# Side work in other places of the order, small steps and element-wise passes on GpSimd, q kept once

## The chip, the cores and the metric

The kernel runs on one core of a Trainium2 chip. The metric is the time on the device of one execution, in microseconds (us). It was measured three times: 1782.32, 1785.84 and 1788.01 us. The engines are TensorE (PE in the profile; PEld is its weight load), VectorE (DVE), ScalarE (ACT), GpSimd (POOL) and SyncE (SP), which here only issues DMAs.

## The reference

Two attention layers follow each other on x of shape (8, 256, 32, 32). N is 1024 positions, C is 256 channels.

```python
# layer 0: 8 heads of 32 channels, one bias matrix per head, residual
xn = (x - mean) / sqrt(var + eps) * gamma            # over the channels
q, k, v = split(w_qkv @ xn)
sim  = einsum('bhdi,bhdj->bhij', q, k) * scale + bias   # bias: a small MLP on relative positions
attn = softmax(sim, axis=-1)
x = w_out @ einsum('bhij,bhdj->bhdi', attn, v) + x
# layer 1: one head, f and g of 32 channels, h of 256
f, g, hh = Wf @ x + bf, Wg @ x + bg, Wh @ x + bh
attn = softmax(f.T @ g, axis=rows)
x = gamma * (hh @ attn) + x
```

## The kernel before, in words

All eight batches are done one after the other, and each in two groups g of four heads. A group has two phases of 32 steps. In its **rows** phase, step m takes one head's tile of 128 queries by 1024 keys. PE computes the tile (lines 581 and 582), DVE adds the bias and takes the minimum of the negated sum (line 1005, the custom instruction with its accumulator read), and ACT exponentiates it for the row sum (line 819). This phase only gives each row's shift: the row's maximum plus the logarithm of its sum. In the **columns** phase, step n computes the scores again, transposed (line 602: 128 keys by 512 queries of two heads), with the shift in two extra rows of `q_stack`. DVE adds the bias (1019), ACT exponentiates (836), and after every two steps PE multiplies with v (629) for the two steps that lie two pairs back.

The four phases of a batch are called g0 rows, g0 columns, g1 rows and g1 columns here. Everything else is **side work**. The tables `side_0`, `column_0`, `side_1` and `column_1` say at which step of which phase each piece is issued, and every engine walks through the same tables (`side_work`), so the order on each engine is fixed by hand. Layer 1 of batch b-1 runs beside batch b, and the normalisation, q and k of batch b+1 too:

- normalisation of the next x: `mean` and `var` on PE (407), `centre` on DVE (863), `square` on ACT (701), `rstd` on ACT (710 the logarithm, 706 the exponential), `norm` on DVE (869);
- q and k: a product on PE (407, 450), a high part rounded by ACT (714, 718, 722, 726) and a low part by DVE (872, 876, 880, 886). The two parts lie in the buffer `st`, go to DRAM (`q_out`, `k_out`) and come back in another layout (`q_in`, `k_in`);
- v: PE (460), copied by ACT (732); output projection `proj`: PE (472), `add_x` on DVE (894);
- layer 1: f and g on PE (407, 484), high on ACT (736, 740), low on DVE (903); h on PE (496), `keep_h` on DVE (931); then per tile `s1` PE (511), `max1` DVE (943), `exp1` ACT (761), `invert` DVE (947), `scale_h` ACT (770) and four `sa` products on PE (527); `add_y` on DVE (954);
- the shift: logarithm and its inverse's exponential on ACT (748, 750), six small instructions of 128x16 on DVE (913 to 925), a transposition on PE (`turn`, 566), a copy on ACT (`keep_rows`, 756) and two small DMAs (341).

PSUM has eight banks. Score tiles take pairs of them in turn: banks 0 and 2 in rows phases, 0, 2 and 6 in columns phases. Bank 4 and 5 hold side work and the sums with v. Before the first step lies a setup (bias MLP, the bias lines through DRAM, q and k of batch 0), and behind the last a tail: layer 1 of batch 7 alone.

## Time and profile before

| what | value |
|---|---|
| median of three executions | 1785.84 us |
| the profiled execution | 1790.26 us |
| its span, first to last instruction | 1788.5 us |
| setup, up to the first DVE step | 98.5 us |
| batch 0; batches 1 to 6 together; batch 7 | 187.7; 1236.8; 194.8 us |
| tail | 70.7 us |
| mean granted TensorE clock | 0.934 |

The profiled execution took 1.8 us more than its span. It lies 4.4 us above the median. Boundaries of phases are the starts of the DVE's first step in each.

### The profile page before, as it was taken

How to read it: one execution, taken by the hardware profiler on the slowest of the kernel's cores; microseconds unless marked ns; L12 is line 12 of the kernel's file. 1: busy time of each engine (PE TensorE's matmuls, PEld its weight loads, DVE VectorE, ACT ScalarE, POOL GpSimd, SP SyncE). 2: the span in 40 equal slices, each digit the busy share in tenths (PEclk: the TensorE clock that was granted, in tenths of full speed). 3: DMA queues.
4: the chain of work that ended last, by engine and by line, in shares of the span. 5: the costliest groups of instructions: out<-in, count | busy, mean ns of one | idle time of the engine just before them, and what ended most of it. 6: DMA issues, size and time to landing. Idle time of an engine off the chain costs nothing.

```text
span 1788.5 us, 18614 instructions
## 1 busy us (share of the span) xinstructions
PE 1589.6 (89%) x5976; PEld 753.9 (42%) x5976; DVE 1477.8 (83%) x2168; ACT 1382.2 (77%) x2033; POOL 7.1 (0%) x5
## 2 busy tenths in 40 slices
PE   6078899899998999889998999989998999999988
PEld 2043335345353544435453443535444453535424
DVE  3067988898988989898888989899889989899853
ACT  2067889788888878878787888878798887889743
POOL 1000000000000000000000000000000000000000
PEclk9577869999999999999999999999999999999999
DMA  5941204320350203501151203502043203400100
GB/s 129 248 138 36 59 1 132 93 59 1 100 148 1 60 1 107 142 25 35 48 165 37 59 1 107 142 1 60 25 124 101 60 1 90 136 1 0 39 10 23
DMA packets 57257, 122.71 MB, mean 69 GB/s; under 512 B 21428, under 2 KB 22964, under 8 KB 57160
## 3 DMA queue, kind: packets, MB, share of 16 engines
q1 hardware_dynamic: 54344, 115.37, 23.5%
q10 hardware_dynamic: 2816, 6.16, 1.3%
q8 instruction: 47, 0.77, 0.2%
q14 instruction: 50, 0.41, 0.1%
HBM read 78.92 MB, written 44.13 MB: 69 GB/s over the span
## 4 chain that ended last, share of the span: by engine, by line
PE 51%; DVE 24%; issue 18%; DMA 3%; ACT 3%; DVEq 0%; ACTq 0%; SPq 0%
DVE biased L1005 13%; PE psum L527 9%; PE psum L602 9%; PE psum L629 8%; PE psum L581 6%; PE psum L407 6%; DVE biased L1019 5%; PE psum L582 4%; PE psum L450 4%; DMA q_stack<-q_parts 2%; PE psum L460 2%; PE psum L484 1%; ACT probs L836 1%; DVE probs L931 1%; DVE x L954 1%
## 5 line engine op out<-in xcount | busy, mean ns | idle before, releaser
L1005 DVE CUSTOM_DVE_ANT_0 biased<-psum,bias_lines_sb 128x1024 f32<-128x1024 f32 x512 | 617.1, 1222 | 174.1 <-PE psum L582 163.0
L819 ACT ACTIVATE biased<-biased,nmax 128x1024 f32<-128x1024 f32 x512 | 587.4, 1148 | 162.5 <-DVE nmax L1005 157.9
L836 ACT ACTIVATE probs<-biased 128x1024 f32<-128x1024 f32 x512 | 536.8, 1057 | 128.6 <-DVE biased L1019 107.5
L1019 DVE TENSOR_TENSOR biased<-psum,bias_lines_sb 128x1024 f32<-128x1024 f32 x512 | 597.8, 1216 | 45.7 <-PE psum L602 33.4
L602 PE MATMUL psum<-q_stack,k_stack 98*128 98x512 f32 x1024 | 392.8, 490 | 38.5 <-DVE nmax L1005 15.9
L581 PE MATMUL psum<-k_stack,q_stack 96*128 96x512 f32 x512 | 331.1, 647 | 102.5 <-DMA q_stack<-q_parts 46.8
L602 PEld LDWEIGHTS psum<-q_stack,k_stack 98*128 98x128 f32 x1024 | 178.9, 200 | 328.8 <-issue 150.8
L629 PE MATMUL psum<-probs,vT 128*32 128x512 f32 x2048 | 285.1, 627 | 6.2 <-DVE st L886 3.9
L581 PEld LDWEIGHTS psum<-k_stack,q_stack 96*128 96x128 f32 x512 | 100.0, 195 | 287.1 <-DVE nmax L1005 165.8
L582 PE MATMUL psum<-k_stack,q_stack 96*128 96x512 f32 x512 | 210.8, 412 | 0.0
L527 PE MATMUL psum<-probs 128*128 128x512 f32 x384 | 186.6, 592 | 0.0
L582 PEld LDWEIGHTS psum<-k_stack,q_stack 96*128 96x128 f32 x512 | 102.7, 201 | 50.7 <-issue 47.4
L819 ACT ACTIVATION_READ_ACCUMULATOR biased<-biased,nmax 128x1 f32 x512 | 96.0, 188 | 0.0
L450 PE MATMUL psum<-xn,wqkvT 128*128 128x512 f32 x128 | 76.9, 694 | 21.4 <-DVE st L880 7.8
L527 PEld LDWEIGHTS psum<-probs 128*128 128x128 f32 x384 | 72.5, 189 | 46.0 <-issue 36.1
L629 PEld LDWEIGHTS psum<-probs,vT 128*32 128x32 f32 x2048 | 42.6, 109 | 101.3 <-issue 73.5
L761 ACT ACTIVATE probs<-probs,nmax 128x1024 f32<-128x1024 f32 x48 | 54.9, 1144 | 16.4 <-DVE probs L943 15.6
L407 PE MATMUL psum<-xn,wqkvT 128*128 128x512 f32 x128 | 66.3, 599 | 0.0
L460 PE MATMUL psum<-wqkvT,xn 128*128 128x256 f32 x256 | 65.7, 378 | 0.0
L496 PE MATMUL psum<-whT,x 128*128 128x256 f32 x256 | 65.4, 380 | 0.1
L472 PE MATMUL psum<-o,woutT 128*128 128x512 f32 x128 | 64.4, 592 | 0.8 <-ACT o L782 0.8
L527 PE MATMUL psum<-o,probs 128*128 128x512 f32 x128 | 64.8, 592 | 0.0
(78 smaller groups left out, 1090.9 us busy)
## 6 DMA issues: line engine op xcount, KB each, us to landing
q_stack<-q_parts SPq DMA_DIRECT2D x90, 256.0 KB, 5.3
k_stack<-k_parts SPq DMA_DIRECT2D x45, 512.0 KB, 7.3
q_parts<-st SPq DMA_DIRECT2D x15, 1024.0 KB, 3.9
k_parts<-st SPq DMA_DIRECT2D x15, 1024.0 KB, 4.3
xn<-in_x_dram SPq DMA_DIRECT2D x8, 1024.0 KB, 8.9
x<-in_x_dram SPq DMA_DIRECT2D x8, 1024.0 KB, 9.6
out_dram<-x SPq DMA_DIRECT2D x8, 1024.0 KB, 4.1
bias_lines_sb<-bias_lines SPq DMA_DIRECT2D x32, 240.0 KB, 15.1
```

The lines of the kernel that those rows point to most:

```text
L407: mm = pe.matmul(psum[0:rows, bank + half, :], lhsT(k), src[:, k, half * HALF:(half + 1) * HALF], start=(k == 0), stop=(k == KC - 1))
L450: mm = pe.matmul(psum[:, bank, :], wqkvT[:, k, t * C:t * C + P], xn[:, k, half * HALF:(half + 1) * HALF], start=(k == 0), stop=(k == KC - 1))
L460: mm = pe.matmul(psum[:, 4 + arg % 2, 0:C], xn[:, k, arg * P:(arg + 1) * P], wqkvT[:, k, 2 * C:3 * C], start=(k == 0), stop=(k == KC - 1))
L527: mm = pe.matmul(psum[:, 4 + 2 * c + half, :], hs[:, t % HS, c * P:(c + 1) * P], attn1[t % 3][:, half * HALF:(half + 1) * HALF], start=(t ...
L581: pe.matmul(psum[:, bank, :], lhsT, keys[:, 0:HALF], start=True, stop=True)
L582: pe.matmul(psum[:, bank + 1, :], lhsT, keys[:, HALF:N], start=True, stop=True).then_inc(SEMS["a_mm"], 1)
L602: mm = pe.matmul(psum[:, bank + i, :], k_stack[:, g, 2 * j + i, t * P:(t + 1) * P], q_stack[:, g, half, 2 * j + i, :], start=True, stop=True)
L629: mm = pe.matmul(psum[h * HD:(h + 1) * HD, 4 + half, :], vT[:, t, (g * HG + h) * HD:(g * HG + h + 1) * HD], probs[:, ((q - PV_LAG) * HP + ...
L819: nc.scalar.activation(biased[:, m % BIASED, :], biased[:, m % BIASED, :], ACT.Exp, scale=-1.0, bias=nmax[:, m:m + 1], accum_out=rowsum[:, ...
L836: nc.scalar.activation(probs[:, n % P_SLOTS], biased[:, n % BIASED, :] .rearrange("p (i n) -> p i n", i=2), ACT.Exp).then_inc(SEMS["probs_ ...
L1005: nc.vector.tensor_tensor_reduce(biased[:, m % BIASED, :], pair(bank_of(g, first, ("rows", m))), bias_lines[:, g * HG + h, a0:a0 + N], -1. ...
L1019: nc.vector.tensor_tensor(biased[:, n % BIASED, :].rearrange("p (i n) -> p i n", i=2), psum[:, bank:bank + 2, :], bias_lines[:, g * HG + 2 ...
```

## The change

- **GpSimd takes over** the six small shift instructions but the rounding, which DVE keeps: four GpSimd instructions stand before it (a fused one is split in two) and two behind it. It also takes `norm`, and the bias of h (`keep_h`), which ACT now copies out of PSUM first.
- **Two new GpSimd steps** add the two halves of x's channels and of the squares, so that `mean` and `var` each need 2 products of 512 columns and not 4.
- **q of group 1, k of group 1, f, `centre` and the logarithm of the variance** are done in halves of 512. k of group 1 is computed one batch ahead. `st` is now `st_q` and `st_k`. `q_stack` is held once and not once per group; its halves are loaded apart, each as soon as the scores before it have been read.
- **High and low parts** stand one step apart; before, it was two (three for `low_g`).
- **The rows phase of g0** has three pairs of banks for its scores (0, 2, 6). A table `SIDE_BANK` gives every piece of side work its bank, and it waits for the piece that had the bank before.
- **h** is in the last steps of g0 rows, in g0 columns and at the start of g1 rows. Its products fill a bank in pairs, its copy takes 512 columns, and `scale_h` writes in place. `s1` comes every 3 steps from step 3, before it was every 8/3 steps from step 6.
- **In g0 columns** the squares are at steps 0 and 1, `var` at 7 and 10, the norm at 12, the first copy of h at 0 and g at 2, 3, 13 and 14. In g1 columns stand the second half of k of group 0 and all of q of group 0 and k of group 1: five products of two steps each, where there were two. The rounding of the shift is at step 4 and its transposition at step 8 (before 6 or 7).
- **In the setup** the bias lines of heads 2 to 7 are no longer loaded ahead of q and k of batch 0, but behind them.

```diff
+        side_0 += [(11 + a, "q1", a) for a in range(QUANTA)]
+        side_0 += [(12 + 2 * half, "high_q1", half) for half in range(NHALF)]
+        side_0 += [(13 + 2 * half, "low_q1", half) for half in range(NHALF)]
-            at = 6 + 8 * t // 3
+            at = 3 + 3 * t
...
+            slots = S_SLOTS if g == 0 else 2
-            banks = [(0, 2)[(n - columns) % 2] for n in range(columns)]
+            banks = [(0, 2, 6)[(n - columns) % slots] for n in range(columns)]
...
+        def q_in(eng, b, g, half):
             need(eng, "q_stored", b, 16 * (g + 1))
-            need(eng, *done)
+            need(eng, "s_mm", b - 1 + g, (SN if g == 0 else 0) + (half + 1) * (SN // NHALF))
...
+            lines_out(0)
+            bias_in(0)
+            bias_in(1)
+            lines_out(1)
+            for half in range(NHALF):
+                need(sp, f"q_loaded_{half}", 0, Q_DMAS)
+            need(sp, "k_loaded", 0, K_DMAS)
+            bias_in(2)
+            bias_in(3)
+            k_out(sp, 0, 1)
+            k_in(sp, 0, 1)
+            for h in range(HG, G * HG):
+                bias_in(h)
...
+                    nc.scalar.copy(hT[:, 2 * arg:2 * arg + 2, :],
+                                   psum[:, SIDE_BANK["h", arg, b], :]
+                                   .rearrange("p (t c) -> p t c", c=C)).then_inc(SEMS["h_kept"], 1)
...
+            def do(kind, arg, b, g):
+                if kind == "sum_x":
+                    nc.gpsimd.tensor_tensor(x_sum, xn[:, 0, :], xn[:, 1, :], ALU.add).then_inc(SEMS["x_summed"], 1)
+                elif kind == "sum_squares":
+                    nc.gpsimd.tensor_tensor(square_sum, squares[:, 0, :], squares[:, 1, :],
+                                            ALU.add).then_inc(SEMS["squares_summed"], 1)
+                elif kind == "norm":
+                    nc.gpsimd.tensor_tensor(xn[:, arg, :], xn[:, arg, :], rstd, ALU.mult).then_inc(SEMS["normed"], 1)
+                elif kind == "shift":
+                    u = g * NHALF + arg
+                    cols = slice(arg * HM, (arg + 1) * HM)
+                    need(pool, "ln_ready", b, 2 * u + 2)
+                    nc.gpsimd.tensor_tensor(invsum[:, cols], rowsum[:, cols], invsum[:, cols],
+                                            ALU.mult).then_inc(SEMS["scaled"], 1)
+                    need(pool, "scaled", b, 3 * u + 1)
+                    nc.gpsimd.tensor_tensor(lnsum[:, cols], lnsum[:, cols], invsum[:, cols],
+                                            ALU.add).then_inc(SEMS["scaled"], 1)
+                    need(pool, "scaled", b, 3 * u + 2)
+                    nc.gpsimd.tensor_scalar(lnsum[:, cols], lnsum[:, cols], -1.0, None,
+                                            ALU.add).then_inc(SEMS["scaled"], 1)
+                    need(pool, "scaled", b, 3 * u + 3)
+                    need(pool, "a_max", b, g * A_TILES + (arg + 1) * HM)
+                    nc.gpsimd.tensor_tensor(shift[:, cols], nmax[:, cols], lnsum[:, cols],
+                                            ALU.subtract).then_inc(SEMS["shifted"], 1)
+                elif kind == "split_shift":
+                    u = g * NHALF + arg
+                    cols = slice(arg * HM, (arg + 1) * HM)
+                    need(pool, "split_hi", b, u + 1)
+                    need(pool, "shift_mm", b, u - 1)
+                    nc.gpsimd.tensor_copy(shift_parts[:, arg, 0], shift_hi[:, cols].bitcast(F32))
+                    nc.gpsimd.tensor_tensor(shift_parts[:, arg, 1], shift[:, cols], shift_hi[:, cols].bitcast(F32),
+                                            ALU.subtract).then_inc(SEMS["parts_ready"], 1)
+                elif kind == "keep_h":
+                    need(pool, "h_kept", b, arg + 1)
+                    nc.gpsimd.tensor_tensor(hT[:, 2 * arg:2 * arg + 2, :], hT[:, 2 * arg:2 * arg + 2, :], bh_all[:],
+                                            ALU.add).then_inc(SEMS["h_ready"], 1)
...
+                elif kind == "round_shift":
+                    need(dve, "shifted", b, u + 1)
                     nc.vector.tensor_copy(shift_hi[:, cols], shift[:, cols]).then_inc(SEMS["split_hi"], 1)
```

DVE at the start of the g0 columns of a middle batch, before:

```order
L1019 TENSOR_TENSOR biased<-psum,bias_lines_sb 128x1024 x4
L869 TENSOR_TENSOR xn<-xn,o 128x1024
L1019 TENSOR_TENSOR biased<-psum,bias_lines_sb 128x1024
L913 TENSOR_TENSOR invsum<-rowsum,invsum 128x16
L916 SCALAR_TENSOR_TENSOR lnsum<-invsum,lnsum 128x16
L919 TENSOR_TENSOR shift<-nmax,lnsum 128x16
L922 CAST shift_hi<-shift 128x16
L924 COPY shift_parts<-shift_hi 128x16
L925 TENSOR_TENSOR shift_parts<-shift,shift_hi 128x16
L1019 TENSOR_TENSOR biased<-psum,bias_lines_sb 128x1024 x3
L903 SCALAR_TENSOR_TENSOR fg_stack<-psum,bfg,fg_stack 32x512
```

And now, up to the end of that phase (L1137 is the old L1019, L1040 the old L903, L1048 the rounding):

```order
L1137 TENSOR_TENSOR biased<-psum,bias_lines_sb 128x1024 x5
L1048 CAST shift_hi<-shift 128x16
L1137 TENSOR_TENSOR biased<-psum,bias_lines_sb 128x1024
L1040 SCALAR_TENSOR_TENSOR fg_stack<-psum,bfg,fg_stack 32x512
L1137 TENSOR_TENSOR biased<-psum,bias_lines_sb 128x1024 x11
L1040 SCALAR_TENSOR_TENSOR fg_stack<-psum,bfg,fg_stack 32x512
L1137 TENSOR_TENSOR biased<-psum,bias_lines_sb 128x1024 x15
```

The norm and five of the small instructions are gone from DVE, and so are the two low parts of k that followed in this phase; the first low part of g comes after 6 steps instead of 8.

PE at the last steps of the g0 rows of a middle batch, before (L581 and L582 are the scores, L407 the mean of squares, which is `var`):

```order
L581 MATMUL psum<-k_stack,q_stack 128x512
L582 MATMUL psum<-k_stack,q_stack 128x512
L407 MATMUL psum<-x,wfgT 96x512
L407 MATMUL psum<-st,mean_w 128x512
L581 MATMUL psum<-k_stack,q_stack 128x512
L582 MATMUL psum<-k_stack,q_stack 128x512
L407 MATMUL psum<-st,mean_w 128x512
L581 MATMUL psum<-k_stack,q_stack 128x512
L582 MATMUL psum<-k_stack,q_stack 128x512
L407 MATMUL psum<-st,mean_w 128x512
```

And now (L665 and L666 are the scores, L573 f, L520 the mean of x, L586 h):

```order
L573 MATMUL psum<-x,wfgT 96x512
L665 MATMUL psum<-k_stack,q_stack 128x512
L666 MATMUL psum<-k_stack,q_stack 128x512
L520 MATMUL psum<-st_k,mean_w 128x512
L665 MATMUL psum<-k_stack,q_stack 128x512
L666 MATMUL psum<-k_stack,q_stack 128x512
L520 MATMUL psum<-st_k,mean_w 128x512
L665 MATMUL psum<-k_stack,q_stack 128x512
L666 MATMUL psum<-k_stack,q_stack 128x512
L586 MATMUL psum<-whT,x 128x256 x2
```

`var` has left this phase for the g0 columns, the mean stands in its place with half the products, and the first products of h are here.

SP from the storing of the bias table on, before:

```order
L369 DMA bias_lines<-bias_table 8064x1x32 x2
L357 DMA bias_lines_sb<-bias_lines 32x1920 x32
L297 DMA q_parts<-st 128x2x1024
L310 DMA q_stack<-q_parts 32x4x512 x6
L381 DMA xn<-in_x_dram 128x2x1024
```

And now:

```order
L436 DMA bias_lines<-bias_table 8064x1x32
L429 DMA bias_lines_sb<-bias_lines 32x1920 x8
L436 DMA bias_lines<-bias_table 8064x1x32
L429 DMA bias_lines_sb<-bias_lines 32x1920 x8
L388 DMA k_parts<-st_k 128x2x1024
L395 DMA k_stack<-k_parts 32x4x1024 x3
L429 DMA bias_lines_sb<-bias_lines 32x1920 x16
L374 DMA q_parts<-st_q 128x2x1024
L463 DMA xn<-in_x_dram 128x2x1024
```

Twenty-four of the 32 loads of bias lines moved behind the loads of q and k, which ACT issues, and so they now stand in front of the store of q for group 1 and the load of the next x.

## Rows read from the trace of the kernel before

**Rows 1.** The page: each engine's busy time, share of the span and instructions.
```profile
PE 1589.6 (89%) x5976; PEld 753.9 (42%) x5976; DVE 1477.8 (83%) x2168; ACT 1382.2 (77%) x2033; POOL 7.1 (0%) x5
```
**Rows 2.** Windows: the four phases of batch 3 in order (clock and DMA last).
```profile
699.90:754.80 54.90, 50.05 (x169) 27.71 (x165) 47.13 (x79) 45.79 (x81) 0.00 (x0) 1.00 0.43 116
754.80:802.10 47.30, 42.22 (x196) 16.76 (x196) 43.27 (x45) 37.89 (x44) 0.00 (x0) 0.96 0.04 14
802.10:862.30 60.20, 58.26 (x193) 32.20 (x192) 51.62 (x103) 52.04 (x92) 0.00 (x0) 1.00 0.15 35
862.30:905.30 43.00, 40.23 (x188) 15.32 (x188) 41.37 (x45) 35.65 (x39) 0.00 (x0) 0.92 0.37 111
```
**Rows 3.** Groups of instructions in g0 rows of batch 3 (busy, mean ns | idle).
```profile
L1005 DVE CUSTOM_DVE_ANT_0 biased<-psum,bias_lines_sb 128x1024 f32<-128x1024 f32 x32 | 38.5, 1221 | 7.6 <-PE psum L582 7.0
```
**Rows 4.** Timeline, g1 rows of batch 3: step 10, and steps where PE is late.
```profile
818.56 1.22 DVE L1005 CUSTOM_DVE_ANT_0 biased<-psum,bias_lines_sb 128x1024 f32<-128x1024 f32 x1
...
824.13 0.39 PE L582 MATMUL psum<-k_stack,q_stack 96*128 96x512 f32 x1
824.36 1.88 PE L527 MATMUL psum<-probs 128*128 128x512 f32 x4
824.67 1.22 DVE L1005 CUSTOM_DVE_ANT_0 biased<-psum,bias_lines_sb 128x1024 f32<-128x1024 f32 x1 [0.68 <-PE psum L582]
...
825.93 1.15 ACT L819 ACTIVATE biased<-biased,nmax 128x1024 f32<-128x1024 f32 x1 [0.67 <-DVE nmax L1005]
826.31 0.39 PE L582 MATMUL psum<-k_stack,q_stack 96*128 96x512 f32 x1
```
**Rows 5.** Timeline: start of g0 columns of batch 3.
```profile
757.27 2.02 ACT L836 ACTIVATE probs<-biased 128x1024 f32<-128x1024 f32 x2
760.37 1.21 DVE L869 TENSOR_TENSOR xn<-xn,o 128x1024 f32<-128x1024 f32 x1
761.50 1.22 DVE L1019 TENSOR_TENSOR biased<-psum,bias_lines_sb 128x1024 f32<-128x1024 f32 x1
762.64 0.16 DVE L913 TENSOR_TENSOR invsum<-rowsum,invsum 128x16 f32<-128x16 f32 x1
763.63 3.48 DVE L1019 TENSOR_TENSOR biased<-psum,bias_lines_sb 128x1024 f32<-128x1024 f32 x3
```
**Rows 6.** Timeline: ACT's high, DVE's low, in g1 columns of batch 3.
```profile
887.05 0.58 ACT L722 ACTIVATE st<-psum 128x512 fp32r<-128x512 f32 x1
888.77 0.68 DVE L880 SCALAR_TENSOR_TENSOR st<-psum,st 128x512 fp32r<-128x512 f32 x1
889.36 15.92 DVE L1019 TENSOR_TENSOR biased<-psum,bias_lines_sb 128x1024 f32<-128x1024 f32 x14
```
**Rows 7.** GpSimd's longest and a short instruction (timeline).
```profile
0.34 0.11 POOL L1099 MEMSET const-uint8-127<- 128x1 uint8 x1
0.74 6.92 POOL L852 MEMSET k_stack<- 2x8192 f32 x1 [0.29 <-POOLq L1099]
```
**Rows 8.** The chain that ended last, setup.
```profile
51.69 14.38 DMA q_parts<-st
68.36 28.51 DMA q_stack<-q_parts
```
**Rows 9.** DMA between 38 and 97 us.
```profile
DMA packets 11740, 14.18 MB, mean 240 GB/s; under 512 B 9052, under 2 KB 9052, under 8 KB 11740
bias_lines_sb<-bias_lines SPq DMA_DIRECT2D x32, 240.0 KB, 15.1
```
**Rows 10.** Timeline: the tail's f and g.
```profile
1728.67 3.67 PE L407 MATMUL psum<-x,wfgT 128*96 128x512 f32 x8 [0.78 <-DVE x L894]
1738.99 3.73 PE L484 MATMUL psum<-x,wfgT 128*96 128x512 f32 x4 [1.55 <-DVE fg_stack L903]
```
**Rows 11.** Windows: batches 1 to 6; g1 rows of batch 0.
```profile
286.20:1523.00 1236.80, 1149.63 (x4465) 554.45 (x4464) 1100.28 (x1614) 1029.93 (x1518) 0.00 (x0) 0.97 0.24 67
202.40:246.70 44.30, 36.46 (x82) 15.11 (x81) 38.79 (x71) 38.83 (x68) 0.00 (x0) 0.59 0.20 46
```

606 lines of the change are left out of this document (330 added, 276 removed).

## The prediction

> **What bounds the kernel now.** I read the page first. PE is busy for 89% of the span, DVE for 83%, ACT for 77% and GpSimd for 7 us in all [rows 1]. No engine is full, so shares alone decide nothing. Next the windows of one steady batch [rows 2]. The reader is to see that its four phases differ. g0 rows take 54.9 us with DVE busy for 47.1. g0 columns take 47.3 with DVE busy for 43.3. g1 rows take 60.2 with PE busy for 58.3, and g1 columns 43.0 with DVE busy for 41.4. In g0 rows DVE's row tiles stood idle for 7.6 us, 7.0 of them behind PE's score tile [rows 3]. The timeline of g1 rows shows the same in detail: from one score tile to the next PE needs 2.18 us (824.13 to 826.31), because two `sa` products lie between, and DVE waits 0.68 us for a tile that costs it 1.22 [rows 4]. So the rows phases are held by PE's side work and by a ring of only two bank pairs, the columns phases by DVE.
>
> Prices come from distances between starts. A score tile in the columns costs DVE (15.92-0.09)/14 = 1.13 us, a low part of 512 columns 0.59 (888.77 to 889.36) [rows 6]. ACT takes 0.96 for a column step (two in 2.02, one of which ends 1.06 after its start) [rows 5]. A norm, like any pass of DVE over 1024 columns, takes 1.13 (760.37 to the next step at 761.50), the six shift instructions 0.99 (762.64 to 763.63) [rows 5]. A row step takes about 1.15 on DVE and on ACT when nothing is late [rows 4]. On PE, eight passes of 512 columns in float32 take 3.67 us with the last one's end, 0.44 each; a product of 512 columns is two passes, 0.88 [rows 10]. A pass of the scores takes half of that, 0.23 (824.13 to 824.36, the next product being on the spot), a tile of two 0.46 [rows 4].
>
> **The change, phase by phase, for a batch in the middle.**
>
> *g0 rows, 54.9 us.* PE loses 10 products of 512 columns (q and k had 8 and q now has 4; mean and var had 8 and the mean now has 2) and gains two tiles of h, 0.88 each: 8.8 - 1.8 = 7.0 us less, 43.1 of busy time instead of 50.1 [rows 2, 10]. Three bank pairs let it run one tile further ahead. DVE loses a low part (two of 1024 columns become two of 512, -1.1 us) and the shift but the rounding (-0.8), and pays 0.3 for f and `centre` in halves: 47.1 - 1.6 = 45.5. The work of PE no longer outlasts it, so I let the 7 us behind PE go. What is late next is ACT: a low part now stands one step behind its high part, not two. DVE's next row tile ends 1.15 us after the last, but ACT needs the 1.15 of its own exponential and then about 0.6 for the high part [rows 6], which leaves DVE some 0.7 us of idle time. There are four such places here (two of q, two of f), 2.8 us. 45.5 + 2.8 + 0.4 = 48.7.
>
> *g0 columns, 47.3 us.* DVE loses two norms (2.3), 0.8 of the shift and two halves of k (1.2): 43.3 - 4.3 = 39.0. ACT gains two squares (1.9 at 0.95 each by the distance of rows 5), three copies of h (1.4 at the 0.5 of a 512-wide instruction) and loses two high parts (1.1): 37.9 + 2.2 = 40.1. PE's passes sum to 38: scores 14.3, v 14 x 0.88, and 10.5 for g, `var`, half of k and four tiles of h, 0.9 for the next row tiles. So all three come close together. The first steps decide. ACT does two exponentials, a copy and two squares before its third exponential, GpSimd then adds the squares, and PE waits at step 7 for the low part of g before it may write `var` into the same bank. I count 5 us of stops over the phase (before: 47.3 - 43.3 = 4): 39.0 + 5 = 44.
>
> *g1 rows, 60.2 us.* Six of the eight tiles of h (5.3 us) have left PE here, and DVE loses `keep_h` (8 of some 0.3, by the 0.59 of twice the width) and 0.8, and gains half a low part of k. The `sa` products stay: 32 x 0.88 = 28.2 us, now over 25 steps instead of 22. PE's work from the first `sa` on is 25 x 0.46 + 28.2 + six `s1` at 0.46 = 42.4, and the old stretch (41.0 by the same sum, 22 steps) took 43.7, from 818.6 to 862.3 [rows 2, 4]. With the same 2.7 on top, 45.1. The seven steps ahead of it, with two `max1` and one low part, are nine DVE instructions of 1.15, 0.6 and one wait: 11.7. Sum 56.8; the end of one and the start of the other overlap, so I take 56.
>
> *g1 columns, 43.0 us.* DVE gains three halves (1.8) and loses 0.8; five low parts now come one step after the high part, up to 0.5 us each, and PE has 3 more products in pairs of neighbouring steps. 43.0 + 1.0 + 2.5 = 46.5 if nothing overlaps; 46.
>
> Sum 194.7 against 205.4 [rows 2]. I take 11 us off each batch, 66 for batches 1 to 6 [rows 11]. Batch 7 has no next x but the same g1 rows: 12.
>
> **GpSimd.** The trace has only memsets of it. The long one writes 8192 elements in 6.92 us, 0.84 ns each; the short one takes 0.11 us [rows 7]. A pass over 1024 elements with two inputs thus lies between 0.86 us (as one write) and 6.9 (the longest row). I take three operands at the write's rate, 2.6 us, and 0.3 for the small ones. All of it fits beside: a batch gives GpSimd 4 long, 4 half and 24 small ones, some 23 us of 195. DVE waits for it at one place, the rounding. In g0 columns that comes after five steps (5.9 us), and GpSimd needs the copy of h at 2.8, its bias (1.3) and four small ones: 5.3. It holds as long as a small one costs under 0.45 us. At 1 us each, DVE waits 2 us there and nothing elsewhere (eight steps lie in between in the rows): 7 x 2 = 14 us. The Trainium skill, "GPSIMD Engine Reference", section "Engine selection", says to keep element-wise work of two inputs on VectorE since GpSimd takes about twice as long; its figures would make the long pass 2.4 us, and the sum would be the same.
>
> **Setup and batch 0.** The first DVE step waits for q at 96.9 us; before it lie 14.4 us of q's store and 28.5 of its load [rows 8]. Between 38 and 97 us the queues moved 14.18 MB at 240 GB/s without a pause, and 24 of the 32 bias loads, 24 x 0.246 = 5.9 MB, now come later [rows 9]. 8.3 MB at the same rate are 34.5 us, so the first step is at about 74, 24 us earlier. A part is paid back: the rest of the bias lines (needed from step 8) and k of group 1 now stand in front of the next x, and the mean of x may wait for it. I put 54 us for g0 rows of batch 0 instead of 57.6, and 3 less over the others: 30 us for setup and batch 0 together.
>
> **Tail.** f and g now run through instead of waiting for their low parts. Their eight products are worth 7.0 us and took 14.1 before, from 1728.67 to 1742.72 [rows 10]. PE then waits about 2 us for the first `scale_h`, since fewer tiles of h stand before it. 5 us.
>
> **Sum.** 66 + 12 + 30 + 5 = 113. 1788.5 - 113 = 1675.5 us of span, 1677.3 as a profiled execution. That execution lay 4.4 us above the median, so I say 1673.
>
> **Rivals.** *(a) The waits move.* In the batches the one-step low parts and ACT's heavy start of g0 columns cost as much as PE's relief gives, so that a batch gains 3 us: 18 + 4 + 30 + 5 = 57 us, 1729. For it: ACT is already at 52.0 of 60.2 in g1 rows and gets more [rows 2]. Against it: in both rows phases it is PE that DVE waits for [rows 3, 4].
> *(b) The setup gives nothing*, since lines of 128 bytes (9052 of 11740 packets) and not megabytes fill the queues, and batch 0 then waits for its bias lines: 1673 + 27 = 1700.
> *(c) Slower: GpSimd and DVE hold each other.* While a GpSimd instruction reads SBUF, DVE's stands still. 23 us x 7 = 160, so 1835. It decides from 113/7 = 16 us a batch, that is if over two thirds of GpSimd's time hits DVE. DVE's long instructions have one input in PSUM and one in SBUF [rows 3]. The Trainium skill, "SBUF — State Buffer", section "Who interferes with whom", has GpSimd blocked by and blocking only DVE instructions with two SBUF inputs or in a 2-port mode. By it nothing here but the 16-column rounding is concerned, and no row of before can show it.
> *(d) PE's clock.* In g1 rows of batch 0, with scores alone, the granted clock was 0.59 [rows 11]. g0 rows lose PE work. At that clock PE's 43 us would be 73, 24 more than the phase I expect; if two thirds of the phase ran so, +16 a batch, 1785, no change. But 43 of 48.7 us is still a fuller PE than batch 0's.
>
> **How the numbers follow.** Forecast 0.62, with a range of its own of 1640 to 1705 (GpSimd's bound, 14 us; stops counted, 3 us in each of 7 batches; the setup, 8). (a) 0.15, (b) 0.11, (c) 0.06, (d) 0.03; 0.03 for a mixture near no change. 0.3% (5 us) is about what a measurement of this kernel can tell. Faster are the forecast, (a) and (b), 0.88; same 0.05; slower 0.07, that is (c) and a bad case of the mixture. The range reaches from 1635, a little below the forecast's own, to (a), 1730.
>
> **What would show it.** Right: the first DVE step near 74 us; windows near 49, 44, 56 and 46; DVE's idle time behind PE in g0 rows under 2 us, and GpSimd's long pass near 2.5. Wrong: ACT's high parts named before DVE's low parts for over 10 us a batch; DVE tiles longer than 1.22 us while GpSimd works; the rounding waiting for GpSimd; the second half of `q_stack` (loaded only after the last scores of the group before) holding PE at row step 16.

## The result: slower by 6%, and the profile after

The change makes the kernel slower: 1900.76 us in the median (1888.75 to 1903.40, 4 runs) beside 1786.71 (1782.32 to 1788.01, 4 runs), a ratio of 1.063 with a 95% interval of 1.058 to 1.068. The prediction was 1673.

The page of the changed kernel is to be set beside [rows 1]. DVE has 31 us less to do, ACT 8 more, and PE's busy time has grown by 54 with 56 fewer matmuls. The second line is the granted clock in 40 slices of the span, in tenths; its mean is 0.898, where it was 0.934.

```profile
PE 1643.6 (86%) x5920; PEld 773.3 (41%) x5920; DVE 1446.6 (76%) x1970; ACT 1389.8 (73%) x2065; POOL 155.2 (8%) x257
PEclk9768698899979999789998899889998899998999
```

The windows of the four phases of batch 3 go with [rows 2], and the last row, batches 1 to 6, with [rows 11] (columns: span, busy time of PE, PEld, DVE, ACT and POOL with their instructions, granted clock, DMA share, GB/s).

```profile
720.80:777.10 56.30, 48.20 (x154) 28.41 (x151) 45.72 (x78) 43.01 (x77) 3.62 (x7) 0.88 0.36 99
777.10:836.40 59.30, 50.14 (x211) 20.24 (x210) 41.38 (x36) 40.37 (x48) 12.21 (x12) 0.88 0.08 21
836.40:896.70 60.30, 56.70 (x170) 29.13 (x168) 49.43 (x91) 51.40 (x94) 2.57 (x7) 0.94 0.03 7
896.70:949.50 52.80, 46.41 (x208) 18.02 (x208) 43.26 (x43) 37.85 (x43) 1.28 (x6) 0.94 0.41 126
263.40:1635.50 1372.10, 1208.46 (x4420) 574.12 (x4416) 1078.81 (x1465) 1035.86 (x1543) 118.10 (x192) 0.91 0.21 61
```

The loss is in the columns phases: group 0's take 59.3 us instead of 47.3 and group 1's 52.8 instead of 43.0, while the two rows phases, where I expected the gain, stand at 56.3 (54.9) and 60.3 (60.2). Over the span it adds up: batches 1 to 6 take 1372.1 instead of 1236.8 us (+135.3); the first row step starts at 64.3 instead of 98.5 and batch 0 takes 11.4 longer (-22.8 together); batch 7 takes 197.5 instead of 194.8 (+2.7); what lies behind it 67.6 instead of 70.7 (-3.1). The sum is +112.1, which is 1900.6 less 1788.5. So the steady batches lost more than the whole kernel did, and the setup hides a part of it.

In the 228.7 us of batch 3 PE was busy for 201.5 and stood for 27.3; before it was 190.8 and 14.6 of 205.4 [rows 2]. About half of the 23 us lost in a batch is standing. The other half is busy time, at a lower clock and with no more matmuls.

What DVE and PE wait for in group 0's columns is in the list of waits of that phase (columns: us in total, times, longest).

```profile
DVE biased L1137 <- PE psum L686: 16.0, 11, 2.9
PE psum L526 <- DVE fg_stack L1040: 3.1, 1, 3.1
PE psum L586 <- ACT o L869: 2.6, 1, 2.6
PE psum L586 <- ACT hT L828: 0.8, 1, 0.8
PE psum L573 <- ACT o L791: 0.8, 1, 0.8
```

DVE waits for PE, 16.0 us; and PE waits, not for data but for banks. L526 is the product of `var` 0, which writes bank 5, and bank 5 is free only when DVE's low part of g (L1040) has read it. L586 is `h` 2, which writes bank 4, where ScalarE's copy of the first half of o (L869) still reads. The timeline shows one such place from its cause to its effect.

```profile
813.23 0.73 PE L686 MATMUL psum<-q_stack,k_stack 98*128 98x512 f32 x2
815.90 0.57 ACT L869 COPY o<-psum 128x512 f32<-128x512 f32 x1
816.52 1.35 PE L586 MATMUL psum<-whT,x 128*128 128x256 f32 x4 [2.56 <-ACT o L869]
817.31 1.41 PE L686 MATMUL psum<-q_stack,k_stack 98*128 98x512 f32 x2
818.52 1.91 PE L586 MATMUL psum<-whT,x 128*128 128x256 f32 x4
818.76 1.23 DVE L1137 TENSOR_TENSOR biased<-psum,bias_lines_sb 128x1024 f32<-128x1024 f32 x1 [2.73 <-PE psum L686]
821.71 1.06 ACT L926 ACTIVATE probs<-biased 128x1024 f32<-128x1024 f32 x1 [4.28 <-PE psum L705]
822.27 2.36 DVE L1137 TENSOR_TENSOR biased<-psum,bias_lines_sb 128x1024 f32<-128x1024 f32 x2 [2.28 <-PE psum L686]
```

PE reaches column step 22 at about 813.9, ahead of DVE, and finds `h` 2. Bank 4 is released by a copy that stands at ScalarE's step 21, and ScalarE comes to it at 815.90. PE works in order, so the score tiles behind `h` 2 stand as well; its lead is gone. DVE then stops twice, for 2.73 and 2.28 us, and ScalarE for 4.28. In the kernel before, the next user of bank 4 was the second half of `k0` at step 24, two steps later, and the trace has no wait of PE's for that copy there.

And the clock goes with it. Windows of 5 us of the same batch:

```profile
772.00:777.00 5.00, 5.00 (x14) 3.96 (x14) 2.24 (x4) 0.97 (x1) 0.00 (x0) 0.57 0.00 0
782.00:787.00 5.00, 2.13 (x12) 0.77 (x12) 4.97 (x4) 4.77 (x6) 3.05 (x5) 0.96 0.00 0
787.00:792.00 5.00, 4.72 (x12) 1.20 (x12) 2.48 (x3) 2.19 (x3) 0.00 (x0) 0.50 0.00 0
792.00:797.00 5.00, 5.00 (x16) 1.86 (x16) 2.45 (x2) 3.20 (x5) 0.00 (x0) 0.52 0.03 7
812.00:817.00 5.00, 2.44 (x14) 0.91 (x13) 4.03 (x4) 4.78 (x6) 0.00 (x0) 1.00 0.00 0
817.00:822.00 5.00, 5.00 (x20) 2.87 (x19) 1.23 (x1) 0.72 (x2) 0.00 (x0) 0.66 0.00 0
```

Behind each stretch in which PE was busy for only 2.13 or 2.44 us of 5, its granted clock is 0.50 or 0.66: part or all of the stretch at 1.2 GHz instead of 2.4. PE then fills its windows or nearly so, and DVE is busy for half of them or less. If the stop is what brings the clock down, 2.6 us of it cost more than themselves; no run here separates the two.

One more row stood out, DVE's rounding beside GpSimd's sum of squares:

```profile
782.82 2.38 POOL L953 TENSOR_TENSOR st_k<-st_k 128x1024 f32<-128x1024 f32 x1 [0.43 <-ACT st_k L785]
783.04 2.19 DVE L1048 CAST shift_hi<-shift 128x16 fp32r<-128x16 f32 x1
```

It converts 16 columns and took 2.19 us here, 2.0 to 2.19 in each of the 7 batches that have a sum of squares, and 0.17 in its 25 other places. It ends when the GpSimd instruction does.

### The profile page after: what moved, and what is told of

It is laid out like the page before. It is cut to its first block, busy times and chain, and to the rows that moved or that the text cites. A ratio compares the mean times of both kernels' runs of the same rounds, so it can differ in the third digit from the quotient of the medians.

```text
span 1900.6 us, 18755 instructions
## 1 busy us (share of the span) xinstructions
PE 1643.6 (86%) x5920; PEld 773.3 (41%) x5920; DVE 1446.6 (76%) x1970; ACT 1389.8 (73%) x2065; POOL 155.2 (8%) x257
## 4 chain that ended last, share of the span: by engine, by line
PE 48%; DVE 21%; ACT 13%; issue 13%; DMA 3%; SPq 1%; DVEq 0%; ACTq 0%; POOL 0%
DVE biased L1123 10%; PE psum L686 8%; PE psum L615 8%; PE psum L705 8%; ACT biased L909 7%; DVE biased L1137 7%; PE psum L536 5%; PE psum L665 4%; PE psum L666 3%; PE psum L586 3%; PE psum L559 2%; PE psum L573 2%; DMA xn<-in_x_dram 2%; ACT probs L926 1%; PE psum L526 1%
## 5 line engine op out<-in xcount | busy, mean ns | idle before, releaser
L1137 DVE TENSOR_TENSOR biased<-psum,bias_lines_sb 128x1024 f32<-128x1024 f32 x512 | 603.4, 1219 | 171.9 <-PE psum L686 167.3
L665 PE MATMUL psum<-k_stack,q_stack 96*128 96x512 f32 x512 | 359.9, 703 | 48.5 <-DVE nmax L1123 23.6
L666 PE MATMUL psum<-k_stack,q_stack 96*128 96x512 f32 x512 | 220.0, 430 | 0.0
L615 PE MATMUL psum<-probs,hT 128*128 128x512 f32 x384 | 207.5, 640 | 6.6 <-ACT hT L857 6.6
L665 PEld LDWEIGHTS psum<-k_stack,q_stack 96*128 96x128 f32 x512 | 106.6, 208 | 214.6 <-DVE nmax L1123 106.1
L666 PEld LDWEIGHTS psum<-k_stack,q_stack 96*128 96x128 f32 x512 | 108.5, 212 | 67.3 <-issue 63.2
L586 PE MATMUL psum<-whT,x 128*128 128x256 f32 x256 | 86.6, 474 | 39.0 <-ACT o L869 17.9
L615 PEld LDWEIGHTS psum<-probs,hT 128*128 128x128 f32 x384 | 77.4, 204 | 49.5 <-issue 33.3
L705 PEld LDWEIGHTS psum<-probs,vT 128*32 128x32 f32 x2048 | 41.4, 110 | 128.3 <-issue 94.9
L573 PE MATMUL psum<-x,wfgT 128*96 128x512 f32 x128 | 72.6, 658 | 13.0 <-DVE x L1031 7.8
L963 POOL TENSOR_TENSOR invsum<-rowsum,invsum 128x16 f32<-128x16 f32 x32 | 7.1, 223 | 928.5 <-ACT invsum L839 928.5
L586 PEld LDWEIGHTS psum<-whT,x 128*128 128x128 f32 x256 | 57.8, 233 | 61.5 <-ACT o L869 21.0
L986 POOL TENSOR_TENSOR hT<-hT,bh_all 128x512 f32<-128x512 f32 x32 | 41.0, 1280 | 507.7 <-ACT hT L828 507.7
L536 PEld LDWEIGHTS psum<-xn,wqkvT 128*128 128x128 f32 x256 | 47.9, 203 | 71.8 <-issue 64.9
```

The costliest lines, as they stand in the source:

```text
L536: mm = pe.matmul(psum[:, bank, :], wqkvT[:, k, t * C + gg * P:t * C + (gg + 1) * P], xn[:, k, half * HALF:(half + 1) * HALF], start=(k == ...
L573: mm = pe.matmul(psum[0:KS, bank, :], wfgT[:, k, ("f", "g").index(kind), :], x1[:, k, half * HALF:(half + 1) * HALF], start=(k == 0), stop ...
L586: mm = pe.matmul(psum[:, bank, odd * C:(odd + 1) * C], x1[:, k, arg * P:(arg + 1) * P], whT[:, k, :], start=(k == 0), stop=(k == KC - 1))
L615: mm = pe.matmul(psum[:, bank, :], hT[:, t, c * P:(c + 1) * P], attn1[t % 3][:, half * HALF:(half + 1) * HALF], start=(t == 0), stop=(t == ...
L665: pe.matmul(psum[:, bank, :], lhsT, keys[:, 0:HALF], start=True, stop=True)
L666: pe.matmul(psum[:, bank + 1, :], lhsT, keys[:, HALF:N], start=True, stop=True).then_inc(SEMS["a_mm"], 1)
```

## The experiments

Two theories were set against each other. **A**: PE waits, in order, for side banks whose last user is released too late, and loses its lead (the clock falling behind it makes it dearer). **B**: GpSimd costs, by holding DVE or by the longer way of the small steps. Times are medians; all ratios are to runs of the kernel before on the same chip, whose median lay between 1784.9 and 1786.7. Phases are those of batch 3; single phases vary from batch to batch, so where it matters the mean of batches 1 to 6 is given too.

| kernel | us | ratio [95%] | g0 rows, g0 columns, g1 rows, g1 columns |
|---|---|---|---|
| before | 1786.7 | 1 | 54.9, 47.3, 60.2, 43.0 |
| after | 1900.8 | 1.063 [1.058, 1.068] | 56.3, 59.3, 60.3, 52.8 |
| x_shift_dve | 1920.0 | 1.076 [1.074, 1.077] | 59.7, 58.2, 59.6, 55.2 |
| x_round6 | 1880.0 | 1.053 [1.050, 1.056] | 55.4, 57.5, 57.6, 54.9 |
| x_copy19 | 1843.6 | 1.032 [1.030, 1.034] | 56.2, 53.3, 60.2, 50.4 |
| x_rows0 | 1884.1 | 1.057 [1.054, 1.060] | 53.6, 58.2, 60.3, 52.8 |
| x_cols0 | 1791.7 | 1.004 [1.003, 1.005] | 56.4, 47.0, 57.6, 51.0 |
| z_all | 1785.4 | 0.999 [0.998, 1.001] | 51.9, 47.2, 59.2, 49.9 |
| x_xfirst | 1782.6 | 0.998 [0.997, 1.000] | 55.5, 47.0, 57.6, 51.0 |
| z_two | 1761.0 | 0.986 [0.984, 0.988] | 53.6, 46.0, 59.3, 49.7 |
| z_less (less work) | 1745.9 | 0.977 [0.975, 0.979] | 53.2, 46.0, 60.2, 47.6 |
| y_small | 1775.0 | 0.994 [0.992, 0.995] | 56.7, 46.3, 60.2, 41.6 |
| y_copy19 | 1783.9 | 0.999 [0.998, 1.000] | 55.0, 48.1, 60.2, 42.3 |
| y_setup | 1759.7 | 0.985 [0.983, 0.987] | 55.1, 46.3, 60.2, 41.4 |

**Is it GpSimd?** x_shift_dve undoes GpSimd's small steps:

```diff
-                    nc.gpsimd.tensor_tensor(invsum[:, cols], rowsum[:, cols], invsum[:, cols],
+                    nc.vector.tensor_tensor(invsum[:, cols], rowsum[:, cols], invsum[:, cols],
...
-                    nc.gpsimd.tensor_copy(shift_parts[:, arg, 0], shift_hi[:, cols].bitcast(F32))
+                    nc.vector.tensor_copy(shift_parts[:, arg, 0], shift_hi[:, cols].bitcast(F32))
```

> The changed kernel, with the small steps from row sums to shift back on VectorE at the same step numbers (four of them a piece become three, and the two that split it). Theory A (TensorE waits for side banks released too late, and loses its lead): the small steps are not what costs, so the time stays near the changed kernel's 1901 us, within 10 us; 32 pieces x 5 small VectorE instructions of some 0.2 us add at most 32 us if VectorE sets the pace. Theory B (the small steps on GpSimd cost, by the port or by their way round): the time falls by 30 us or more. A by itself leaves the long rounding beside GpSimd's sum of squares as it is.

It got 19 us slower, where theory A had said within 10 and theory B 30 faster. So the small steps on GpSimd aren't the loss. How much of the 19 they are worth isn't clean here: the rounding was long in 11 places, not 7, and four of these are in group 0's rows. y_small makes the same edit alone in the kernel before:

> The kernel before, with one part of the change alone: the small steps from row sums to shift on GpSimd (the rounding on VectorE), at the step numbers of the changed kernel; no long GpSimd instruction, nothing else moved. Theory A: the part is harmless, the time is 1787 us within 6, or up to 25 us faster, since some 32 x 5 short VectorE instructions go. Theory B: slower than before by 15 us or more.

11.5 us faster than before (0.994), within theory A's range, and with all roundings short: group 1's columns lost 1.4 us and group 0's 1.0, while group 0's rows took 1.8 more. This is the clean comparison, and these steps gain a little on GpSimd. x_round6 moves the rounding away from GpSimd's long instruction:

```diff
-            side += [(0, "shift", 1), (4, "round_shift", 1), (4, "split_shift", 1), (8, "turn", 1), (7, "keep_rows", 1)]
+            later = 2 if side is column_0 else 0
+            side += [(0, "shift", 1), (4 + later, "round_shift", 1), (4 + later, "split_shift", 1),
+                     (8 + later, "turn", 1), (7 + later, "keep_rows", 1)]
```

> The changed kernel, with the second rounding of group 0 two steps later, when GpSimd's sum of squares should be over (the transpose and its copy two steps later too). Theory B (VectorE and GpSimd hold each other): the rounding falls from 2.19 to 0.17 us in the 7 places, and the time falls by at least 14 us, to 1887 or less, and by up to 40 us if the stops after it were its doing. Theory A: the rounding is short again but group 0's columns still take 57 us or more (59.3 now) and the time falls by under 10 us.

The rounding was short again in all 32 places:

```profile
772.15 2.40 POOL L955 TENSOR_TENSOR st_k<-st_k 128x1024 f32<-128x1024 f32 x1 [0.44 <-ACT st_k L787]
...
777.44 0.17 DVE L1050 CAST shift_hi<-shift 128x16 fp32r<-128x16 f32 x1
```

The kernel gained 20.7 us, which is 3 a batch: theory B's effect is real and near a fifth of the loss. (The edit also moves the transposition and its copy by two steps, and no run separates them.) The phase still took 57.5, as theory A has it; its "under 10 us" was wrong.

**Is it the banks?** x_copy19 changes one number:

```diff
-                        if n == SN // NHALF + (PV_LAG + 1) * HP - 1:
+                        if n == SN // NHALF + PV_LAG * HP - 1:
                             output(b, g, 0, last)
```

> The changed kernel, with ScalarE's copy of the first half of o at column step 19 instead of 21, so that bank 4 comes free before TensorE stands at h 2 (step 22) and k1 0 (step 23). Theory A: TensorE's waits of 2.56 and 2.1 us for the copy go, with VectorE's stops behind them; group 0's columns fall from 59.3 to 55 or less and group 1's from 52.8 to 51 or less, some 5 us a batch, 35 to 45 us in all (1860). Theory B: the copy has nothing to do with the loss, and the time stays within 8 us of 1901.

57 us, from moving a copy of 0.57 us by two steps, more than the 35 to 45 expected. The 7 long roundings were all still there. The same place in its timeline, to set beside the one above:

```profile
791.63 0.57 ACT L869 COPY o<-psum 128x512 f32<-128x512 f32 x1
792.25 1.13 PE L586 MATMUL psum<-whT,x 128*128 128x256 f32 x4 [0.30 <-ACT o L869]
793.03 0.82 PE L686 MATMUL psum<-q_stack,k_stack 98*128 98x512 f32 x2
```

PE waits 0.30 instead of 2.56, and `h` 2 takes 1.13 instead of 1.35 us. y_copy19 is the control, the same edit in the kernel before:

> The kernel before with ScalarE's copy of the first half of o at column step 19 instead of 21, which alone was worth 57 us in the changed kernel. Theory A: in the kernel before no user of bank 4 stands between step 22 and the copy, so the copy's place is worth nothing, 1786 within 5 us. Rival: the copy's place costs by itself (ScalarE or the products of v), and this kernel gets faster by 15 us or more too.

Nothing (0.999): the copy's place costs only when the next user of bank 4 comes too early behind it, at step 22 as the change arranged it and not at 24 as before. x_cols0 adds the other banks of group 0's columns:

```diff
-        column_0 += [(2, "g", 0), (3, "g", 1), (4, "high_g", 0), (5, "low_g", 0)]
-        column_0 += [(7, "var", 0), (8, "ln_var", 0), (10, "var", 1), (11, "ln_var", 1), (11, "rstd", 0)]
+        column_0 += [(2, "g", 0), (3, "g", 1), (3, "high_g", 0), (4, "low_g", 0)]
+        column_0 += [(8, "var", 0), (8, "ln_var", 0), (12, "var", 1), (12, "ln_var", 1), (12, "rstd", 0)]
...
-        column_0 += [(13, "g", 2), (14, "g", 3), (15, "high_g", 1), (16, "low_g", 1)]
-        column_0 += [(22, "h", 2), (23, "h", 3), (24, "keep_h", 1), (26, "h", 4), (27, "h", 5), (28, "keep_h", 2)]
+        column_0 += [(16, "g", 2), (17, "g", 3), (17, "high_g", 1), (18, "low_g", 1)]
+        column_0 += [(23, "h", 2), (24, "h", 3), (24, "keep_h", 1), (27, "h", 4), (28, "h", 5), (28, "keep_h", 2)]
```

> The changed kernel with the copy of o at 19 (43 us less by the last runs' medians: 1844) and, in group 0's columns, g's parts a step earlier (3 and 4), var at 8 and 12, ln_var 8 and 12, rstd 12, g's second half at 16 and 17, h a step later at 23, 24, 27 and 28. Theory A: TensorE's waits for bank 5 (3.14 us behind low_g, 1.3 behind ln_var) go, and group 0's columns fall from about 55 to 50 or less; some 4 us a batch, 1815. Rival (the rounding and GpSimd hold this phase, since the 7 long roundings stay): the time stays within 8 us of 1844.

Another 52 us, nearly twice what theory A had said (the 43 in that text should read 57), and the kernel as a whole is within 0.4% of the one before. The window of group 0's columns, to set beside the second row of the first such fence above:

```profile
740.40:787.50 47.10, 43.48 (x211) 18.47 (x209) 39.28 (x37) 39.93 (x48) 12.21 (x12) 1.00 0.10 26
```

The same 211 matmuls, in 47.1 us instead of 59.3, and the clock is 1.00 all through instead of 0.88. PE's busy time fell by 6.7 us with the same work: that goes with the clock. But two causes are mixed here. In this kernel the rounding was long in only 1 place, by the shifted times and without an edit to it. By x_round6 six short roundings are worth up to 18 us, so between 34 and 52 of the 52 us are the banks'.

The total also hides what is still lost. Batches 1 to 6 take 1268.7 us, which is 103.5 less than in the changed kernel and 31.9 more than before; the first row step, 32 us earlier (66.1), pays for that. The rest lies in group 1's columns: 51.0 us on average instead of 43.1. x_rows0, built on the changed kernel again, treats group 0's rows in the same way:

```diff
-        side_0 += [(22, "sum_x", 0)]
-        side_0 += [(24 + a, "f", a) for a in range(QUANTA)]
-        side_0 += [(25 + 2 * half, "high_f", half) for half in range(NHALF)]
-        side_0 += [(26 + 2 * half, "low_f", half) for half in range(NHALF)]
-        side_0 += [(28 + half, "mean", half) for half in range(NHALF)] + [(30 + half, "centre", half) for half in range(NHALF)]
-        side_0 += [(30 + t, "h", t) for t in range(2)]
+        side_0 += [(19, "sum_x", 0)]
+        side_0 += [(22 + half, "mean", half) for half in range(NHALF)] + [(24 + half, "centre", half) for half in range(NHALF)]
+        side_0 += [(26 + a, "f", a) for a in range(QUANTA)]
+        side_0 += [(26 + 2 * half, "high_f", half) for half in range(NHALF)]
+        side_0 += [(27 + 2 * half, "low_f", half) for half in range(NHALF)]
+        side_0 += [(31, "h", t) for t in range(2)]
```

> The changed kernel, with group 0's rows in another order of side work: mean at 22 and 23 and centre at 24 and 25, ahead of f (26 to 29), GpSimd's sum of x at 19, high_f at 26 and 28, low_f at 27 and 29, h 0 and h 1 at 31. No user of a side bank now stands at TensorE before the step by which its bank's last user is over on VectorE or ScalarE, less two. Theory A (TensorE's waits for side banks): the waits of 2.6 and 3.4 us at the end of the phase go, group 0's rows fall from 56.3 to 51 or less, and with full clock at the start of the columns some 6 us a batch, 45 us in all, go (1855). Rival: the waits move to mean (its sum on GpSimd) and the time stays within 10 us of 1901.

17 us, where 45 were expected. Over batches 1 to 6 the phase fell by 2.5 us on average and the columns behind it by 2.4, a batch by 5.0. Batch 0 took 6 us more (its stop is told below) and the first row step came 3 us later. The new step of the sum of x also laid it beside the other rounding of group 0: 11 of the 32 were long, four more than before the edit. So the direction is theory A's, but its size can't be read from this run: four more long roundings, at some 3 us each by x_round6, hide a part of it.

**Everything together**, z_all (the edits of x_round6, x_cols0 with the copy at 19, x_rows0, and in group 1's columns the high parts one step earlier):

```diff
-            column_1 += [(one, kind, 2 * half), (two, kind, 2 * half + 1), (two + 1, "high_" + kind, half),
+            column_1 += [(one, kind, 2 * half), (two, kind, 2 * half + 1), (two, "high_" + kind, half),
```

> The changed kernel with all of it together: the rounding at 6 in group 0's columns, the copy of o at 19, group 0's rows in the order of mean first, group 0's columns with var later, and in group 1's columns the high parts in the step of their second matmul with the low parts two steps behind. Theory A with B's 2 us a batch on top: batches of about 197 us (49 rows, 47 columns, 57 rows, 44 columns) against 205.4 before and 228.7 in the changed kernel, with the setup's 34 us kept less the 11 us that batch 0 gave back: 1901 less 7 times 30 is 1690. If the loss were GpSimd's or the clock's by itself, it stays above 1800.

115 us less than the changed kernel, but 95 more than expected: no difference from before. A batch takes 208.2 us, not 197. (Its sum of x now lies beside another rounding in some batches, and 4 of the 32 are long again.) Batches 1 to 6 are still 20.6 us behind the kernel before (1257.4), and the setup makes up for it. So bank waits and the long rounding explain most of what the batches lost, and a batch won nothing. Two stretches of z_all say where that went. The first is batch 0, whose rows take 69.5 us. In the changed kernel already (64.1) its timeline reads:

```profile
92.36 0.41 SPq L463 DMA_DIRECT2D xn<-in_x_dram  x1
...
115.64 2.34 POOL L950 TENSOR_TENSOR st_k<-xn 128x1024 f32<-128x1024 f32 x1 [19.85 <-DMA xn<-in_x_dram]
118.03 2.08 PE L520 MATMUL psum<-st_k,mean_w 128*128 128x512 f32 x2 [15.12 <-POOL st_k L950]
```

The next x stands behind the 16 transfers of the bias lines of heads 4 to 7, which are needed only from 169 us on, and PE, in its fixed order, holds every row tile behind the product of its mean. x_xfirst puts x ahead of them, in the kernel of x_cols0:

```diff
-            for h in range(HG, G * HG):
-                bias_in(h)
...
                     sp.dma_start(xn[:], x_dram[b + 1]).then_inc(x_loaded, 16)
+                if first:
+                    for h in range(HG, G * HG):
+                        bias_in(h)
```

> The kernel of x_cols0 (1792 us), with SyncE's 32 transfers of the bias lines of group 1's four heads behind the transfer of the next element's x in the first batch, instead of ahead of it. In the changed kernel that x was issued at 92.36 us, landed at 115.6, and TensorE stood at mean for GpSimd's sum of it until 118.03, VectorE 16.2 us behind it. Theory: batch 0's first rows phase falls from 63.3 us to about 47, so 1776 us (14 to 17 less). Rival: the bias lines, now later, are late for group 1, or the 6 us of other stops in that phase were the transfers' too, and the gain is under 8 us.

The phase fell from 63.3 to 52.9 and the median by 9 us (the ratio from 1.004 to 0.998), between the two cases. The wait partly moved: GpSimd has x at 100.25 now, but the columns' first product waits 8.4 us for the shift rows, whose small transfers stand behind the same bias lines. (16 transfers were moved, four each for four heads; the 32 in the expectation is miscounted.) The other stretch is group 1's columns:

```diff
-        for kind, half, one, two in (("k0", 1, 2, 3), ("q0", 0, 7, 8), ("q0", 1, 13, 14), ("k1", 0, 23, 24),
+        for kind, half, one, two in (("k0", 1, 5, 6), ("q0", 0, 10, 11), ("q0", 1, 15, 16), ("k1", 0, 23, 24),
```

> The kernel of z_all (1785 us), with the same order of transfers (x of the next element ahead of the bias lines of group 1), k0's second half at 5 and 6 and q0 at 10, 11, 15, 16 in group 1's columns, high_g 4 and low_g 6 and var at 9 in group 0's. Theory: batch 0's first phase falls from 69.5 to 46 us (x's transfer, 23 us), group 1's columns fall from 49.9 to 46, since TensorE no longer makes k0 at half clock with no score tile ahead, and group 0's columns from 47.2 to 45.5: 1785 less 23 less 7 times 5 is 1727. Rival: the lead is lost at the start of each columns phase whatever stands there, and only x's 23 us go (1762).

24 us less: 16 by the end of batch 0, which is x's transfer, and 7 in the six batches behind it. Group 1's columns stayed at 49.7 against the expected 46, so moving k0 did not help, and the rival (1762) came nearest. Three of its windows:

```profile
842.00:847.00 5.00, 5.00 (x22) 2.06 (x21) 4.56 (x6) 3.90 (x6) 0.00 (x0) 1.00 0.36 147
857.00:862.00 5.00, 5.00 (x30) 1.95 (x26) 4.55 (x6) 3.83 (x6) 0.00 (x0) 1.00 0.70 206
862.00:867.00 5.00, 5.00 (x23) 1.97 (x26) 4.90 (x5) 4.78 (x6) 0.00 (x0) 1.00 0.60 201
```

PE is full at full clock. That alone proves nothing, since the kernel before shows the same in this phase:

```profile
882.00:887.00 5.00, 5.00 (x30) 2.03 (x26) 4.55 (x5) 4.68 (x5) 0.00 (x0) 1.00 0.00 0
```

But the change had put six matmuls of k into the phase, where DVE and PE had stood close together (41.4 and 40.2 of 43.0 us, [rows 2]). z_less takes three of them out again and so leaves half of the sum out of three halves of k; everything else is kept:

```diff
+                    alone = b > 0 and (kind, half) in (("k0", 1), ("k1", 0), ("k1", 1))
+                    if alone and k > 0:
+                        return
```

> The kernel of z_two (1761 us) with work left out: of k0's second half and of both halves of k1, all three made in group 1's columns, only the first of the two matmuls each is done for batches 1 to 7 (so those keys are half a sum). Three matmuls of 1.02 us less in the phase; VectorE's and ScalarE's work is the same. If TensorE is what bounds group 1's columns (busy 5.00 of every 5 us with the clock at 1.00 there), the phase falls from 49.7 by 3 us or a little more, since one pair is made at half clock (46.5), and the kernel by 7 times 3, to 1740. If it is the waits between VectorE and ScalarE that bound it, the phase stays within 1 us of 49.7 and the kernel at 1758 or above.

The phase fell to 47.6 (2.1 us, and 2.1 on the mean of batches 1 to 6), as PE's busy time in it did (45.5 to 43.4), and the kernel by 15; 0.9 us came back in group 1's rows (60.2; 0.3 on the mean). So PE's work holds this phase. Three of the six matmuls are still in it, and it still takes 4.6 us more than before; what the other three are worth wasn't tried.

**What the setup is worth by itself**, in y_setup, which gives y_small the changed kernel's order of the bias lines, with those of heads 4 to 7 behind x as in x_xfirst:

```diff
+            lines_out(0)
+            bias_in(0)
+            bias_in(1)
+            lines_out(1)
+            need(sp, "q_loaded", 0, Q_DMAS)
+            need(sp, "k_loaded", 0, K_DMAS)
+            bias_in(2)
+            bias_in(3)
```

> The kernel before with the small steps on GpSimd (1775 us) and the order of the bias lines: those of heads 0 and 1, then a wait for the stacks, heads 2 and 3, and heads 4 to 7 behind x of the next element in batch 0. The setup's term by itself: the first row step comes at about 65 us instead of 98.5, some 30 us less, 1745, if nothing in batch 0 waits for a transfer in its place; if batch 0 stops for bias lines or x, 10 us less at most (1765).

The first row step comes at 72.3 instead of 98.7, 26 us earlier, but batch 0's rows take 64.5 instead of 57.4, so batch 0 gives back a quarter of it. The profiled spans differ by 19 us (1773.4 and 1754.3), the medians by 15; the profiled execution was the fastest of four. y_setup and z_two, 1760 and 1761 us, are the fastest complete versions, 1.5 and 1.4% below the kernel before. The first has only two parts of the change and x's earlier place, so the rest of the change brought nothing, even mended.

## Why the prediction was wrong

**What bounds the kernel** was half read. DVE does wait for PE in the rows [rows 3, 4], but I took this for PE's load alone and let "the 7 us behind PE go" once PE had less to do. In the changed kernel they are still there, 8.0 us in group 0's rows, and PE stands in that phase for banks that DVE has yet to read (2.6 and 2.1 us, the longest two).

**g0 columns is the step that failed** (44 forecast, 59.3 measured). I summed the phase by engine (39.0, 40.1, 38) and added "5 us of stops". I had seen that PE "waits at step 7 for the low part of g before it may write `var` into the same bank", put it into the 5 us, and did not ask the same of the other users of banks 4 and 5. The order in which a bank's users stand and the step of each release were all in the change. With those steps mended the same phase took 47.0 and 46.0, so the forecast missed by 15 us and by 2 or 3 of them for other reasons. The missing term was PE in order behind a bank: it is most of the 12 us that this phase lost, of 23 in a batch. The long rounding is some 2 to 3 of them (x_round6). x_copy19 shows it with nothing else changed, 57 us, x_cols0 together with the rounding. That the falling clock carries a part of it rests on the windows alone (PE's busy time 50.1 against 43.5 for the same matmuls), since no run holds the clock and leaves the waits.

Of the three engines in that sum two were right: in x_cols0 DVE was busy for 39.3 us and ACT for 39.9. PE was busy for 43.5 at full clock where I had 38, with a score pass at 0.23 and a product with v at 0.88; the products with v alone were busy for 14.9, not 12.3. (The profile models the ends of matmuls, so its busy times aren't PE at its peak.) The three did not come "close together": PE was the fullest.

**g1 columns** (46 forecast, 52.8 measured, 49.7 with the waits mended) failed twice: by the same waits (3 us), and because I gave k's matmuls no price of their own, only 2.5 us of stops, in a phase that I took to be DVE's. PE was 1.1 us below DVE there. Its 40.2 and six matmuls at my own 0.88 are 45.5, above DVE's 42.4; I never wrote that sum. z_less shows that PE's work counts one for one in this phase; why z_two's 49.7 is another 4 us above that sum is open.

**g0 rows** (48.7 against 56.3): best seen in z_all, at 51.9 in batch 3 and 53.6 on average. There DVE was busy for 45.8 (45.5 forecast), its low parts waited 2.6 us for ACT's high ones (2.8 forecast), and 2.2 us behind PE were left. These terms were right once the order was mended; PE's was not (43.1 forecast, 45.6 at a clock of 0.97). **g1 rows** (56 against 60.3) stayed where they were; six tiles of h left PE, and its busy time fell by only 1.6 us, at a clock of 0.94 instead of 1.00. In x_cols0, with the clock at 1.00, PE was busy for 54.0 and the phase took 57.6.

A check on the whole would have warned me. By [rows 2] PE was busy for 190.8 of 205.4 us, so it stood 14.6; z_two's 208.6 us hold 191.5. I forecast 194.7 with hardly less for PE to do (4 products of `mean` and `var`, 3.5 us), which means that half of PE's stops had to go. No kernel here got there; the least was 14.0, in y_small.

**GpSimd** was right in its prices: 2.38 us for a long pass (2.6 forecast; the estimate of 2.4 by the ratio in the Trainium skill, "GPSIMD Engine Reference", section "Engine selection", comes out), 1.28 for half, 0.20 to 0.25 for the small ones, and DVE never waited for its result at the rounding. Rival (c) was wrong as I priced it (1835 by all of GpSimd's time) and true in one instruction. The Trainium skill, "SBUF — State Buffer", section "Who interferes with whom", names `cast` among the instructions that can take the pair of ports shared with GpSimd, and says that the later one then waits for all of the other. The trace agrees: 2.19 us instead of 0.17, while DVE's score tiles, with one input in PSUM, kept their mean of 1220 ns in a phase with 12.2 us of GpSimd in it. I had written that only "the 16-column rounding is concerned" and gave it no price; it had a long GpSimd pass on top of it in 7 batches, and moving it was worth 3 us each. Of the four signs that were to show the forecast wrong none came: ACT's high parts held DVE's low ones for 3.4 us a batch and not 10, DVE's tiles stayed at 1.22, the rounding never waited, and PE waited for `q_stack` only in the setup. What went wrong was not on the list.

**Rival (d)**, the clock, I had tied to PE's load. In group 0's rows it did fall, from 1.00 to 0.88, but also in group 0's columns, where there are more matmuls than before (0.96 to 0.88). In both it fell behind waits of PE. **Rival (a)**, the waits move, named waits, though between DVE and ACT and not PE's for banks, and at 1729 still made it a gain.

**Setup and batch 0**: the first row step came 34 us earlier, not 24, and batch 0 gave 11 back, not gained 6: 23 against 30. Between 38 and 64 us the queues moved 7.20 MB at 277 GB/s, where I had 8.3 MB at 240. That "the mean of x may wait for it" was the right sentence with no number to it; PE stood there for 15.1 us and DVE for 16.2. **Batch 7**: 3 us more, not 12 less; its group 0's columns took 49.7 us instead of 41.4, and 42.1 in z_two, so it lost in the same phase. **Tail**: 3 us against 5.

## What to carry to other kernels

When side work is moved in an in-order TensorE stream, write down for each PSUM bank its users in order, the step at which TensorE stands at the next one, and the step at which the last one's reader runs; if the reader's step isn't at least TensorE's lead before it, price a stop there, and look for a stretch of slow clock behind it. A sum of busy times cannot see this, and one copy two steps too late was worth 57 us of 1900. Before forecasting a gain from moving work off TensorE, add up its work in each period after the change, at prices from the trace, and look at how long it stands: beyond the work taken away, its standing time is all that such a change can win. And compare the steady batches by themselves. The mended kernels matched or beat the old one only because a shorter setup hid the 14 to 36 us that batches 1 to 6 still lost.

## What the runs showed of the hardware

- A DVE conversion of 16 columns, float32 to the rounded form, took up to 2.19 us beside GpSimd's sum of two SBUF operands (2.38 us) and 0.17 otherwise; DVE's bias additions beside GpSimd's work, with one input from PSUM, kept 1.22.
- The granted clock fell to 0.50 for 3 to 10 us at a time. In the two places shown it did so behind waits: TensorE had been busy for 2.1 and 2.4 of the 5 us before, at a clock of 0.96 and 1.00. Batch 3 of the kernel before has two such stretches, that of the changed kernel six.
- A transfer of x issued behind 16 of bias lines on the same queue landed 23 us after its issue (92.36 to 115.6); put ahead of them, GpSimd had it 8.4 us after (91.89 to 100.25).
